# Local attention layers: the inverse norm by a power on GpSimd and one Newton step, and the first tile's scores, maximum and exponentials moved behind the last projection

## The reference, cut to what matters

```python
def l2norm(t):
    return t / jnp.clip(jnp.linalg.norm(t, axis=-1, keepdims=True), 1e-12)

def _layer(x, wqkv, qs, ksc, wo, lg, lb, w1, b1, w2, b2):
    h = shift_token(x)                       # second half of the channels from the token before
    q, k, v = split(h @ wqkv, 3)             # 128 -> 3 x 512, as 8 heads of 64
    q = l2norm(q) * qs
    k = l2norm(k) * ksc
    q, k = rotary_xpos(q, k)
    o = local_attention(q, k, v)             # softmax over the own and the previous window of 64
    x = x + o @ wo
    h = layernorm(shift_token(x)) * lg + lb
    a, g = split(h @ w1 + b1, 2)
    return x + (a * gelu(g)) @ w2 + b2
for l in range(DEPTH):
    x = _layer(x, ...)
```

## Time and profile before

| | us |
|---|---|
| median of 3 runs | 2490.08 (2489.07 to 2490.46) |
| the profiled execution | 2490.05 |
| its span, first to last instruction | 2488.1 |
| granted TensorE clock over the span | 0.934 of full |

### The profile page before, as it was taken

How to read it: one execution, slowest core, us unless ns; L and a number is a source line. 1 busy time by engine, 2 the same in 40 slices (tenths; PEclk the granted TensorE clock), 3 DMA queues, 4 the chain that set the end, 5 groups by cost and what they waited for, 6 DMA issues and landing times.

```text
span 2488.1 us, 48854 instructions
## 1 busy us (share of the span) xinstructions
PE 2087.6 (84%) x18320; PEld 1228.3 (49%) x18320; DVE 1937.4 (78%) x4231; ACT 1424.7 (57%) x2618; POOL 600.0 (24%) x480
## 2 busy tenths in 40 slices
PE   5997789787799688978789958987788995888876
PEld 3674233556467323355647723336464772334645
DVE  7756997887755799788785579977878458997786
ACT  4343577748334377784733437767563343776765
POOL 2632000432253100134134210021505330004050
PEclk9998899999899799999989969999998996999999
DMA  4002100100000210011000030010100003001010
GB/s 155 1 1 64 41 11 6 34 21 19 18 1 1 77 31 8 15 26 32 16 9 1 1 90 20 7 27 16 32 13 9 1 5 87 20 10 35 5 33 21
DMA packets 63892, 63.25 MB, mean 25 GB/s; under 512 B 22000, under 2 KB 49200, under 8 KB 63152
## 3 DMA queue, kind: packets, MB, share of 16 engines
q1 hardware_dynamic: 60472, 57.27, 9.2%
q10 hardware_dynamic: 3192, 2.90, 0.4%
HBM read 24.68 MB, written 15.01 MB: 16 GB/s over the span
## 4 chain that ended last, share of the span: by engine, by line
PE 41%; DVE 37%; ACT 15%; issue 5%; DMA 1%; SPq 0%; DVEq 0%; ACTq 0%
PE PS L1388 40%; DVE arena L1136 18%; ACT arena L750 9%; DVE arena L1236 2%; DVE s_at L1211 1%; DVE arena L1204 1%; DMA tmp<-xf 1%; ACT arena L697 1%; DVE tmp L1211 1%; PE PS L1406 1%; ACT arena L758 1%; DVE arena L1329 1%; ACT arena L718 1%; ACT tmp L704 1%; ACT arena L720 1%
## 5 line engine op out<-in xcount | busy, mean ns | idle before, releaser
L1388 PE MATMUL PS<-arena 128*32 128x256 f32 (+5 forms) x11328 | 797.6, 325 | 165.5 <-DVE arena L1136 72.2
L1388 PEld LDWEIGHTS PS<-arena 128*32 128x32 f32 (+5 forms) x11328 | 368.6, 118 | 594.9 <-DVE arena L1136 293.0
L1136 DVE TENSOR_REDUCE arena<-PS 128x1 f32<-128x512 f32 x1024 | 639.5, 683 | 18.7 <-PE PS L1388 18.2
L697 ACT ACTIVATE arena<-PS 128x1024 f32<-128x1024 f32 x512 | 519.1, 1028 | 196.7 <-PE PS L1388 196.3
L652 ACT ACTIVATE arena<-PS 128x512 f32<-128x512 f32 x256 | 150.7, 597 | 245.2 <-PE PS L1388 245.0
L1388 PEld LDWEIGHTS PS<-w2e,arena 128*128 128x128 f32 x2048 | 246.0, 192 | 50.0 <-issue 49.7
L1098 DVE TENSOR_TENSOR arena<-PS,arena 128x512 f32<-128x512 f32 x128 | 86.4, 689 | 214.5 <-PE PS L1388 214.1
L1388 PE MATMUL PS<-w2e,arena 128*128 128x128 f32 x2048 | 247.5, 275 | 0.1
L750 ACT ACTIVATE arena<-PS,arena 128x128 f32<-128x128 f32 x512 | 236.4, 626 | 0.0
L503 POOL TENSOR_TENSOR zz<-zz,arena 128x512 f32<-128x512 f32 x104 | 135.1, 1299 | 271.3 <-DVE arena L1098 242.8
L1388 PE MATMUL PS<-wqkv,arena 128*128 128x512 f32 x384 | 176.8, 598 | 21.7 <-ACT arena L732 21.7
(11 more groups left out here) (306 smaller groups left out, 3267.0 us busy)
## 6 DMA issues: line engine op xcount, KB each, us to landing
arena<-arena SPq DMA_DIRECT2D x120, 128.0 KB, 2.3
scr_q<-arena SPq DMA_DIRECT2D x40, 128.0 KB, 2.4
scr_k<-arena SPq DMA_DIRECT2D x40, 128.0 KB, 2.4
arena<-scr_k SPq DMA_DIRECT2D x24, 200.0 KB
arena<-scr_q SPq DMA_DIRECT2D x24, 192.0 KB
scr_m<-arena SPq DMA_DIRECT2D x256, 1.0 KB
x_in<-in_x SPq DMA_DIRECT2D x5, 512.0 KB, 4.7
arena<-scr_m SPq DMA_DIRECT2D x128, 2.0 KB
```

The costliest lines, as they stand in the source:

```text
L697: act.activation(pb[:, n % 8], pair(2 * (n % 2)), ACT.Exp).then_inc(S["p"], 1)
L1136: dve.tensor_reduce(mxp[:, blk % 2, j, t, hf:hf + 1], PS[:, ring_bank(m), :], AX, ALU.max)\
L1388: return pe.matmul(o, w, v, start=start, stop=stop, **kw)
```

## The change

It does two things. The inverse norm: Pool computes the sums of squares to the power of -0.5 (32 columns, the exponent from a column `sc[:, 13:14]`), ScalarE's Sqrt and VectorE's reciprocal go; the Newton step stays, and takes the power as its start. Pool issues the power after the addition of tiles 2, 4 and 6 and after the last one (t = 8), ahead of the product of tile t - 2. And the order: TensorE does scores(0) behind qkv(7) and ahead of kq(3); VectorE does top(0) behind rotate(7) and ahead of inverse(4); ScalarE does tile 0's exponentials behind the V copy of tile 7 and ahead of keep(3). ScalarE's dummy exponential stays only in the second layer of a sample, behind tile 1. The buffers of the exponentials count by the tile in the layer and no more by the running tile.

```diff
@@ Pool
-            pool.wait_ge(S0["dve0"], 2)
+            pool.wait_ge(S0["dve0"], 3)
...
+                        if t >= 2 and t % 2 == 0:
+                            pool.wait_ge(S["ssq_ok"], u // 2)
+                            pool.tensor_tensor(rq[:, t - 2:t], rqt[:, t - 2:t],
+                                               bc(sc[:, 13:14].broadcast_to([P, 2 * HL]), [P, 2, 2 * HL], 1), ALU.pow)\
+                                .then_inc(S["rq0"], 1)
                         if t >= 2:
                             k = u - 2
+                            pool.wait_ge(S["rq0"], k // 2 + 1)
                             pool.wait_ge(S["rot"], k + 1)
                             pool.wait_ge(S["rqe"], k + 1)
@@ ScalarE
+                    def weights(u):
+
+                        n = T * l + u
+                        act.wait_ge(S["ml"], n + 1)
+                        if n >= 3:
+                            act.wait_ge(S["pt_ps"], 2 * (n - 2))
+                        for r in range(2):
+                            for c in range(4):
+                                h = 2 * c + r
+                                act.activation(pl[:, u % 3, r, c], PS[:, 2 * (n % 2) + r, KEYS * c:KEYS * c + KEYS],
+                                               ACT.Exp, bias=ml[:, n % 2, r, c:c + 1], scale=rq[:, u, h:h + 1],
+                                               accum_out=sl[:, u % 3, r, c:c + 1]).then_inc(S["p_exp"], 1)
+
                     for t in range(T + LAG + 1 - LATE):
...
-                        if 2 <= t <= T and t % 2 == 0:
-                            k = t - 2
-                            act.wait_ge(S["ssq_ok"], u // 2)
-                            act.activation(rq[:, k:k + 2], rqt[:, k:k + 2], ACT.Sqrt).then_inc(S["rq0"], 1)
-                        if t == T:
+                        if t == T - 1:
+                            weights(0)
+                        if l and t == 1:
                             act.activation(sc[0:1, 9:10], ident[0:1, 0:1], ACT.Exp)
@@ VectorE
+            link(dve.memset(sc[:, 13:14], -0.5))
...
                         dve.wait_ge(S["rq0"], (l * T + k) // 2 + 1)
-                        link(dve.reciprocal(y, y))
                         link(dve.scalar_tensor_tensor(w, y, -0.5, y, ALU.mult, ALU.mult))
...
                         if t < T:
                             rotate(t)
+                        if t == T - 1:
+                            top(0)
...
-                    top(0)
                     inverse(T - 2)
@@ TensorE
                         if l == 0 and t == 3:
                             pe.wait_ge(S["op_rd"], 1)
+                        if t == T - 1:
+                            scores(0)
                         if t >= LAG:
                             kq(t - LAG)
                     for t in range(EARLY):
-                        scores(t)
+                        if t:
+                            scores(t)
                         kq(T - LAG + t)
```

More of the change, by code:

```diff
@@ L740, in _ @@
                         n = T * l + u
[L741 to L742 removed]
+                        if 1 <= u < T:
+                            if u <= LATE:
                                 keep(T - LATE + u - 1)
[L744 to L752 removed]
+                            weights(u)
                         if 2 <= u <= T + 1:
@@ L1276, in _ @@
                             dve.wait_ge(S["p_exp"], 8 * (m + 1))
[L1277 to L1279 removed]
+                            link(dve.reciprocal(rl[:, (u - 2) % 3], sl[:, (u - 2) % 3]))
+                            v = pl[:, (u - 2) % 3]
+                            dve.tensor_tensor(v, v, bc(rl[:, (u - 2) % 3], [P, 2, 4, KEYS], 3), ALU.mult).then_inc(S["pn"], 1)
                         if 1 <= u < T:
```

36 lines of the change are left out of this document (11 added, 25 removed).

## The result

| | us |
|---|---|
| before | 2490.27 (2489.07 to 2490.82) |
| after | 2627.02 (2626.55 to 2628.85) |
| ratio | 1.055, 95% interval 1.053 to 1.057 |
| span of the profiled execution after | 2626.7, granted clock 0.914 |

The change makes the kernel 136.7 us slower, 17.1 us for each of the 8 local layers. The forecast was 9.6 us slower.

A forecast was written before the change was run, and what follows sets the result against it. Bound: VectorE through the rotations, then ScalarE's exponentials, so the start of tile 1's exponentials counts. Per layer 0.0 to the last rotation, + 1.2 us after it; times 8, + 9.6 on 2490.08: 2499.7 us, range 2480 to 2528.

The forecast's parts named there:

- Part 1: Layer up to VectorE's last rotation: saved reciprocals and Sqrt gain at most 0.55 us, set against the power on Pool.
- R: Moment VectorE finishes the last rotation of a layer, 570.04 before; forecast 569.5 at best, unmoved with a 1.2 us power.
- p = 1.2 us: Estimated length of one 32-column power on Pool, with 0.25 to 2.4 us kept for the range.
- the 1.2 of the order: From last rotation to tile 1's exponentials: the new order makes this stretch 1.2 us longer in each layer.
- R = 568.8 + p: End of last rotation moves with the power's length, never below 569.5: gain up to 0.55 us, none at 1.2 us.
- W1: Start of tile 1's exponentials on ScalarE, 580.70 before; the layer ends as much later or earlier as this does.
- nothing while p is under 2.5: Last power, ahead of tile 1's maximum, costs nothing below 2.5 us at low clock; at full clock, above 0.5 it would.
- R + 11.85: Forecast start of tile 1's exponentials after the last rotation, TensorE at low clock: 1.2 us later than before.
- Rival 1: Power on Pool short, under 0.9 us, TensorE's clock low: 2492 to 2496 us; chance 22%.
- Rival 2: Power long, Pool becomes the bound: + 15 us at 1.6, + 38 at 2.4, 2504 to 2530 us; chance 22%.
- Rival 3: TensorE's clock holds or is back before scores(1): tile 1's exponentials 1.05 us earlier, about 2484 or 2477 us; chance 15%.
- Rival 4: Tile 0 not brought forward: scores(0) waits, its exponentials start late, total stays near 2490 us; chance 8%.

The follow-up runs named there:

- the two padded runs: Changed kernel with a plain 128x32 product in the power's place, behind one or two idle 128x512 products on Pool: 2505.58 and 2546.35 us.
- the first try: Plain-product kernel with keep(3) first, now without power: last pair's norms on VectorE (integer estimate, three Newton steps), keep(4) also before tile 0's exponentials: 2490.78 us.

## Why the prediction was wrong

**Part 1, the reciprocals and R.** Right: with a short power R came at 569.30, forecast 569.5. The layer began 0.24 us earlier, so 0.5 us are the reciprocals and Sqrt, forecast 0.55.

**p = 1.2 us. This is the step that failed.** The term p, the length of the power on Pool, was put at 1.2 us and measured 5.43. The prediction took a power as "worth 12 to 15 plain operations per column"; measured are 0.159 us a column against some 2.2 ns for a plain one, 72 of them. (The 0.25 us that the prediction reads as the price at the plain rate is the whole row of 0.244; the rate alone gives 0.07 us for 32 columns. Neither changes the term that failed.) The upper bound of 2.4 us was no bound either. It was the longest Pool operation in the trace, of 1024 columns, but a row bounds another operation only from above if something makes that operation the lighter one, and nothing did. A function whose price no row showed should have left the range open upward, or the range should have gone by "what if a column costs 50 or 100 times a plain one".

**How R follows p.** The turn was laid out rightly (power ahead of the product, inverse waiting, no room from the second power on), and the price given for p = 1.6, + 15 us, was met at 1.59 with + 15.2. Its prices for 2.0 and 2.4, + 25 and + 38, are near the straight line between the two padded runs (+ 28 and + 40), though the terms that it shows (p - 1.2, p - 1.15 and the 1.2 of the order, times 8) add up to + 23 and + 29 only; where the rest came from it does not say. The formula R = 568.8 + p, twice over from p = 1.15, was for R alone. At 5.43 it gives + 8.5; from Square 0 to Square 7 it took 9.8 and 11.5 us more.

**R to W1.** Of the last power it was said: "nothing while p is under 2.5". At 5.43 it costs: it ends at 488.70, inverse(6) waits 7.43 us for it, tile 1's maximum stands behind it, and 6.7 us a layer are lost there. The prediction's start of that maximum, R + 7.4 + p, would be R + 12.8; measured is R + 15.1. The third power had already delayed Pool: the last one starts at R + 9.0 here and at R + 6.5 with the plain product. Then the scaling of tile 1's maximum took 1.06 us beside Pool's product and not 0.17.

**The order.** Right in every link: tile 0's exponentials at R + 1.5, kq(4)'s wait of 5.9 us (forecast 5.8), the low clock there, kq at 1.94 us (1.97). The sum was R + 11.85 and came out at R + 10.96 with a short power, since the clock was back in the middle of scores(1); the prediction had that case at 11.1 to 12. The Trainium skill, "TensorE: Matmul & The Clock Gate", section "HAM oscillation — how this bites in real kernels", says that a long wait between groups of matmuls brings the low clock back in every turn of a loop. The trace agrees for this wait of 5.9 us: the clock is 0.50 from 571.1 to 577.9 in this layer, and 0.50 over kq(4) in all eight. What it cost is 1.2 us in the second layers and 1.6 in the first, by the run with TensorE kept busy.

**The rivals.** Rival 1 (short power, 2492 to 2496) is the run with the plain product, 2490.5, just under its range. Rival 2 (Pool bound) is what happened, far past its end of 2530. Rival 3 (W1 = R + 9.6 at full clock) is met at 9.77 when TensorE is kept busy, though the total does not show it. Rival 4 fell.

**The other signs.** Table loads as forecast: 4 instead of 16 for these lines. The range, 2480 to 2528, missed by 99 us, since its bounds of p ended at 2.4.

## What to carry to other kernels

Before moving a function to another engine, find a row of that function on that engine; if there is none, the forecast has no upper end, and one small kernel that runs it at two widths gives the price. An instruction that stands in the middle of another engine's closed turn costs its length several times over, here 4 us a layer for each microsecond. Bringing a consumer forward on one engine can hold back the copy that frees a third engine's banks: ask what each instruction that is jumped over would have released. And a saving of 10 us may not show in the total when stages that the edit did not touch come out longer, here by a lower clock in some and by a late start of TensorE in others; the rows of the stage tell it apart.

## What the runs showed of the hardware

- A power on Pool costs 0.37 us and 0.159 us a column (128 partitions, float32), the same with the exponents -0.5, 0.3, 1.0 and 2.0: 5.42 us for 32 columns.
- VectorE and Pool hold each other up on some instructions. The 128x8 scaling took 0.17 us alone, 2.36 beside Pool's addition of 2.36, and 1.06 beside a product of 1.04 (490.62 in the kernel after); two integer steps of 128x32 took 1.00 and 0.97 and not 0.17 beside Pool; and Pool's product took 2.13 and not 1.04 us (581.25 in the first try) while VectorE multiplied 128x1024 by a row in SBUF. Maxima, sums and rotations, which have one input or read PSUM, ran beside Pool at their usual 1.21 to 1.28. The Trainium skill, "GPSIMD Engine Reference", section 1 "Specifications", says that Pool shares its SBUF interfaces with VectorE and contends with instructions that read two SBUF inputs or run in a two-port mode. The trace agrees beside Pool's sums and products, with these numbers; in which mode the integer steps ran, no run shows. Beside the power it does not: the same scaling took 0.17 us at 475.56 in the kernel after, while a power ran on Pool from 472.62 to 478.05, and a product of 128x1024 from SBUF took its usual 1.22 us (491.64 in the run with other widths) beside the power of 64 columns.
- The same wait of 2.19 us on TensorE is followed by clock 0.57 in one sample and 1.00 in the next. So the time of a stage can change by 1.7 us when all that has changed is when it begins.
- TensorE's first transposes of a sample came after a standstill of 5.1 to 5.2 us at the turn of the loop, and in the run with 6 idle matmuls twice after 9.6 us, with nothing in the profile that held them. The cause is open.
